# Bank tables for every TensorE step and newly found engine orders in a fused Mamba and local-attention kernel

## What is computed

```python
# Mamba: 256 inner channels, 16 states
u = silu(causal_conv4(x @ in_w + in_b))
delta = softplus((u @ dt1_w + dt1_b) @ dt2_w + dt2_b)
h[t] = exp(delta * A) * h[t-1] + ((exp(delta * A) - 1) / A) * B * u     # for 16 states
y = (sum_n C_n h_n + D * u) * silu(x @ gate_w + gate_b)
x = layernorm(x + y @ out_w + out_b)
# twice (layers l = 0, 1), 8 heads of 64, windows of 64 that see themselves and the one before
q, k, v = split(shift(x) @ wqkv)
q, k = rotary(l2norm(q) * qs, l2norm(k) * ks)
x = x + softmax(mask(q @ k.T)) @ v @ wo
h = layernorm(shift(x)) @ w1 + b1
x = x + (a(h) * gelu(g(h))) @ w2 + b2
x = layernorm(x_in + x)
```

## Time and profile before

| what | value |
|---|---|
| runs, us | 1066.7, 1067.91, 1068.65 |
| median | 1067.91 us |
| span of the profiled execution | 1068.3 us |
| PE busy | 929.2 us, 87% |
| DVE busy | 872.8 us, 82% |
| ACT busy | 786.6 us, 74% |
| POOL busy | 695.8 us, 65% |
| mean granted PE clock | 0.954 |

### The profile page before, as it was taken

The page is one execution under the profiler, slowest core; times in us unless marked ns, Lnnn a source line. Parts: engine busy times, 40 slices in busy tenths (PEclk is TensorE's granted clock), DMA queues, the critical chain, the costliest instruction groups (busy, mean ns, idle before and its releaser), DMA issues. The chain is left out here.

```text
span 1068.3 us, 25986 instructions
## 1 busy us (share of the span) xinstructions
PE 929.2 (87%) x10152; PEld 560.7 (52%) x10152; DVE 872.8 (82%) x1244; ACT 786.6 (74%) x1897; POOL 695.8 (65%) x386
## 2 busy tenths in 40 slices
...
DMA packets 22618, 25.63 MB, mean 24 GB/s; under 512 B 2869, under 2 KB 14815, under 8 KB 22495
## 3 DMA queue, kind: packets, MB, share of 16 engines
...
## 5 line engine op out<-in xcount | busy, mean ns | idle before, releaser
L1062 DVE TENSOR_TENSOR_SCAN scan<-du,decay 128x1028 f32<-128x1028 f32 (+1 forms) x160 | 306.3, 1952 | 10.9 <-PE YY L1252 7.3
L768 POOL TENSOR_TENSOR rn<-ssc,expo 128x16 f32<-128x16 f32 x64 | 214.0, 3344 | 5.3
L764 POOL TENSOR_SCALAR ssc<-ss 128x16 f32<-128x16 f32 x64 | 62.4, 975 | 213.4 <-DVE ss L1119 212.8
L914 ACT ACTIVATE prob<-BB,nmax 128x128 f32<-128x128 f32 x472 | 165.7, 380 | 39.4 <-DVE nmax L1157 28.0
L859 ACT ACTIVATE decay<-delta,negA 128x1024 f32<-128x1024 f32 (+1 forms) x160 | 154.2, 986 | 18.4 <-DVE scan L1062 16.5
L773 POOL TENSOR_TENSOR qkc<-qkc,qks 128x1024 f32<-128x1024 f32 x64 | 159.6, 2493 | 2.8 <-DVE qks L1137 2.7
L1252 PE MATMUL YY<-scan,diag 64*64 64x512 f32 (+1 forms) x1280 | 143.1, 538 | 10.9 <-DVE scan L1062 10.9
L777 POOL TENSOR_TENSOR qkc<-qkc,rn 128x1024 f32<-128x1024 f32 x64 | 133.2, 2082 | 5.0
L1252 PE MATMUL AA<-wqkv,hT 128*128 128x512 f32 x256 | 128.8, 627 | 6.0 <-DVE qks L1137 3.1
L914 ACT ACTIVATION_READ_ACCUMULATOR prob<-BB,nmax 128x1 f32 x472 | 104.2, 221 | 0.0
L1119 DVE TENSOR_REDUCE ss<-sq 128x16 f32<-128x1024 f32 x64 | 77.1, 1205 | 29.6 <-ACT sq L877 29.6
...
## 6 DMA issues: line engine op xcount, KB each, us to landing
...
```

The lines of the kernel that those rows point to most:

```text
L768: pool.tensor_tensor(rn[:, q % 2, :], ssc[:, :], expo[:, 0:2 * HEADS], ALU.pow).then_inc(rn_sb, 1)
L914: ins = act.activation(prob[:, h, :], bank_of(q, a)[:, c * P:(c + 1) * P], ACT.Exp, bias=nmax[:, q % 2, h:h + 1], accum_out=den[:, q % 2, ...
L1062: dve.tensor_tensor_scan(state, step, a, 0.0, ALU.add, ALU.mult).then_inc(scan_sb, 1)
```

## The change

Three things are edited.

**Tables of banks.** HOLDS and LATE go. Each PE step of a kind that needs a pair or a single bank is given its own by a letter in a table: A, B or Y for a pair, C or M for a single bank. Y may be taken once the Mamba part is over. All readers (ACT and DVE) address the bank by the same table. Instructions, their sizes and their number stay as they were.

```diff
+PAIR_TABLES = {
+    "qk_in": "ABBAABBBBBBBBBABBABBABBBAAAAAAAABBBBBBBBAAAAAABAAAABBBYAYYYYAABA",
+    "qk_T": "AAAAABBABABABABBBABAABABBBBBBAAAAABBAABBBBAAAABBAABAYBBBABYYBBAB",
...
+BANK_TABLES = {
+    "layer_T": "CMMMCMMCCCMMMMMCCMMM",
...
-LATE = [q for q in range(TILE.index((0, GROUPS - 1, 0)), len(TILE)) if q % 2]
...
-HOLDS = {"qk_in": "A", "qk_T": "B", "scores": "B", "probs_T": "B", "v_in": "C", "weighted": "C", "out_T": "C",
-         "attn_out": "M", "shift": "M", "norm_T": "M", "layer_T": "M", "up_gate": "AM", "up_a": "M", "down": "M"}
-OWN = {"scores": "qk_T", "probs_T": "scores", "out_T": "weighted"}
+SINGLES = {"layer_T": lambda l, g: QUAD.index((l, g)), "up_a": lambda f, c: NCH * f + c}
+PAIR_STEPS = {name: table.split() for name, table in PAIR_TABLES.items()}
+BANK_STEPS = {name: table.split() for name, table in BANK_TABLES.items()}
...
 def banks_of(step, args):
-    banks = HOLDS.get(step, "")
-    return "Y" if banks == "B" and args[0] in LATE else banks
+
+    pairs, banks = PAIR_STEPS.get(step), BANK_STEPS.get(step)
+    n = nth(step, args)
+    return (pairs[0][n] if pairs else "") + (banks[0][n] if banks else "")
+
+
+OWN = {"scores": lambda q: [("qk_T", (q,))], "probs_T": lambda q: [("scores", (q,))], "out_T": lambda q: [("weighted", (q,))],
+       "shift": lambda f: [("attn_out", (f,))], "norm_T": lambda f: [("shift", (f,))],
+       "down": lambda f: [("up_a", (f, c)) for c in range(NCH)]}
...
-    held, last = {}, {}
+    held, last = {}, {"Y": ("mamba_sum", (GROUPS - 1,))}
...
-            def free(step, *args):
-
-                for last, (f, *rest) in HELD[step, args]:
-                    if last == "attn_out":
-                        pe.wait_ge(x2_sb, f + 1)
...
+            def free(step, *args):
+
+                for last, of in HELD[step, args]:
+                    pe.wait_ge(*release(last, *of))
...
             def qk_T(q):
-                if q == LATE[0]:
-                    pe.wait_ge(m_sum, GROUPS)
```

**Orders.** All five order strings are replaced. The steps are the same ones (848 on PE, 654 on ACT, 710 on DVE, 197 on POOL, 89 on SP); where they stand differs. The planner that wrote the new strings took a DVE scan and a POOL tensor operation to exclude each other in time; nothing in the kernel enforces that. The first steps on DVE:

```diff
 DVE_ORDER = """
-differences 0, step_size 0, scan 0 0, scan 0 1, scan 0 2, scan 0 3, scan 0 4, scan 0 5, scan 0 6, scan 0 7,
...
+differences 0, masks 0, step_size 0, tables 0, scan 0 0, scan 0 1, scan 0 2, scan 0 3, scan 0 4, scan 0 5, scan 0 6,
```

More of the change, by code:

```diff
@@ L94 @@
[L94 to L103, removed]
@@ new lines @@
+1, state_y 2 8, weighted 2, attn_out 0, state_y 2 9, state_y 2 10, scores 3, state_y 2 11, shift 0, state_y 2 12,
+state_y 2 13, probs_T 3, state_y 2 14, state_y 2 15, norm_T 0, out_T 2, up_gate 0, up_a 0 0, mamba_out 2, weighted
+3, u_in 3, out_T 3, up_a 0 1, gate_in 3, up_a 0 2, layer_T 0 2, qk_in 4, v_in 4, rank 3, qk_in 5, step_in 3, down 0,
+v_in 5, attn_out 1, qk_T 4, layer_T 1 0, qk_in 6, scores 4, shift 1, v_in 6, skip 3, state_y 3 0, v_in 7, qk_T 5,
+probs_T 4, state_y 3 1, qk_in 7, scores 5, state_y 3 2, state_y 3 3, weighted 4, norm_T 1, qk_T 6, out_T 4, up_gate
@@ new lines @@
+17, down 3, attn_out 4, out_T 12, state_y 4 6, weighted 13, shift 4, probs_T 14, state_y 4 7, scores 15, state_y 4
+8, out_T 13, qk_T 16, state_y 4 9, weighted 14, qk_in 18, norm_T 4, out_T 14, probs_T 15, v_in 17, state_y 4 10,
+v_in 18, scores 16, weighted 15, state_y 4 11, up_gate 4, up_a 4 0, up_a 4 1, state_y 4 12, out_T 15, up_a 4 2,
+probs_T 16, state_y 4 13, down 4, weighted 16, qk_T 17, qk_in 19, state_y 4 14, scores 17, state_y 4 15, attn_out 5,
+mamba_out 4, qk_T 18, shift 5, out_T 16, u_in 5, probs_T 17, scores 18, v_in 19, weighted 17, layer_T 0 4, gate_in
@@ new lines @@
+probs_T 22, out_T 21, state_y 5 7, qk_T 23, qk_in 25, weighted 22, scores 23, down 6, state_y 5 8, state_y 5 9, v_in
+24, out_T 22, probs_T 23, v_in 25, qk_T 24, weighted 23, state_y 5 10, qk_in 26, state_y 5 11, scores 24, out_T 23,
+state_y 5 12, v_in 26, attn_out 7, probs_T 24, state_y 5 13, qk_T 25, qk_in 27, scores 25, state_y 5 14, state_y 5
+15, weighted 24, shift 7, mamba_out 5, probs_T 25, out_T 24, qk_T 26, u_in 6, scores 26, norm_T 7, v_in 27, gate_in
+6, weighted 25, up_gate 7, up_a 7 0, probs_T 26, layer_T 0 5, qk_T 27, out_T 25, qk_in 28, scores 27, v_in 28,
@@ new lines @@
+8, state_y 6 9, v_in 34, state_y 6 10, down 8, out_T 30, probs_T 31, qk_T 32, qk_in 34, state_y 6 11, scores 32,
+weighted 31, state_y 6 12, state_y 6 13, out_T 31, probs_T 32, attn_out 9, state_y 6 14, state_y 6 15, qk_T 33,
+shift 9, qk_in 35, weighted 32, scores 33, mamba_out 6, out_T 32, v_in 35, norm_T 9, qk_T 34, u_in 7, probs_T 33,
+up_gate 9, gate_in 7, weighted 33, scores 34, layer_T 0 6, out_T 33, qk_T 35, up_a 9 0, v_in 36, qk_in 36, rank 7,
+up_a 9 1, up_a 9 2, probs_T 34, step_in 7, down 9, scores 35, qk_in 37, weighted 34, v_in 37, skip 7, probs_T 35,
```

605 lines of the change are left out of this document (299 added, 306 removed).

## The result

| | before | after |
|---|---|---|
| median, us (range) | 1067.7 (1066.7 to 1068.65) | 1025.4 (1022.72 to 1030.71) |
| ratio, 95% interval | | 0.9619 (0.9588 to 0.9651) |
| span of the profiled execution, us | 1068.3 | 1023.9 |
| its mean granted clock | 0.954 | 0.979 |

The kernel became 42 us faster. The forecast was 1033 us, the range 1006 to 1062. The total came out within 8 us, in part by luck: the waits that the sum was made of gave 21 us and not 35, one term had the wrong sign, and the clock, for which the sum had no term, gave about 18 us.

What follows compares the result with a forecast made beforehand. PE was taken as nearest to the bound, nearly co-bound with DVE in the middle, with 41.6 us of bank waits. Terms -25 - 4 - 3 - 0.9 - 2.4 = -35 took 1068.3 to 1033 us, range 1006 to 1062.

Steps and rivals of the forecast that it cites:

- Bank waits: PE steps held by an unreleased pair or bank: 60% of 41.6 us goes, -25 us, between -8 and -42.
- rival A: Freed PE steps only wait for their data instead: bank term -8 instead of -25, 1050 us; chance 0.17.
- qk_T to scores: `scores` waited 5.4 us for its own `qk_T` copy and now stands further behind: -4 us, between 0 and -5.4.
- Scans against POOL: DVE scans and POOL operations exclude each other; an order keeping them apart saves -3 us, between -13 and +5.
- The opening: Table multiplies and casts before the first scan, `qk_in` 0 ahead of group 1's state steps: -0.9 us, between -8 and +7.
- The end: Last GELU to `down`: with C and M in turn, 5.5 us becomes about 3.1: -2.4, between -1 and -3.5.
- the clock: PE matmuls at the upper clock instead of the lower: little to win in the middle (granted 0.99); no term in the sum.
- B: The release compounds: attention fills the opening (-8) and all bank waits go (-42), 1009 us; chance 0.08.
- C: Pairs with scores stay held until their exponentials are done, stopping PE: slower, 1079 us; chance 0.09.
- D: DVE and ACT alone limit the order, bank waits are only where slack shows: time stays at 1068; chance 0.04.
- DVE must do 639 us in 693, 92%: Check on the middle: DVE's load if 20 of the 35 us gained fall there, which it nearly reached before.
- PE's idle time near 105: Sign that the forecast is right: PE's idle time falls to near 105 us, from 139.

Runs made afterwards that it cites:

- tables_only: Kernel before with its old orders, each step given the pair or bank that comes free first (333 of 648 entries differ): 1042.98 us, ratio 0.9775.
- order_only: New orders of after with the old fixed banks wherever these orders can run with them (66 entries still differ): 1089.39 us, ratio 1.0215.
- new_pairs: Kernel after with its table of pairs kept, but single banks C and M fixed by kind as before (29 entries deviate): 1065.98 us, ratio 0.9981.
- new_singles: Kernel after with its table of single banks kept, but pairs A and B fixed by kind as before (37 entries deviate): 1059.21 us, ratio 0.9912.
- tables_tail: Kernel before with its old orders, banks chosen freely only after the last `mamba_out` (87 entries): 1053.57 us, ratio 0.9867.
- tables_mid: Kernel before with its old orders, banks chosen freely only up to the last `mamba_out` (240 entries): 1068.3 us, ratio 1.0009.
- after_short_rotate: Kernel after with POOL's addition and multiply of `rotate` done on only 128 of 1024 columns: 1017.3 us, ratio 0.953.
- after_half_sums: Kernel after with DVE's sums of squares taken over 32 of each head's 64 values: 1031.45 us, ratio 0.9668.

## Why the prediction was right, and where it wasn't

**Bank waits, -25: the right mechanism, its size in part by luck.** tables_only, the nearest to this term by itself, measured -24.7. But the term was counted in PE's idle time, and of that only 14.6 us went there: 20 us of bank waits (46.0 to 25.6), while the rest grew by 6.5, as rival A says in small. The other 10 us are matmuls at the upper clock. In after, the idle time of the eight kinds fell by 18.6 where 25 was forecast. No run shows why it is less. Rival A in full (waits change their name, -8) falls: `probs_T` waits 6.8 us for exponentials, not more than 9.4. The table of runs says the same: with the new orders, bank waits of 70, 52, 48 and 27 us go with 1089, 1066, 1059 and 1025.

**qk_T to scores, -4: right**, 5.4 to 0.7 us.

**Scans against POOL, -3: wrong in sign.** The step that failed is "an order that keeps them apart can save a part of 13 us". The order doesn't keep them apart: 13 us of stretching became 22. It is the order that does it: the scans sum to 315 to 321 us in after, order_only, new_pairs and new_singles, and to 299 to 306 in before, tables_only, tables_tail and tables_mid. With the norms' multiplies and the casts DVE has some 17 us more to do. What that costs in time is bounded by after_short_rotate, about 8 for all 36 us of stretching; an estimate in proportion, 17 / 36 x 8, gives +4, at the upper end of my range (-13 to +5). Besides, PE now waits 21 us more for scans, which no term had; order_only has 20 of them. What the orders gain lies elsewhere, in the rest of PE's idle time, 82.2 us before and 59.1 after, where no term of mine stood. The largest part of that is `norm_T` behind `ffn_norm`, 11.4 to 2.7 us, and order_only has the 2.7 too.

**The opening, -0.9: inside its range (-5 measured, range -8 to +7), by luck.** "The casts fit in DVE's wait for the softplus" is false: they took 2.03 + 0.96 us instead of 0.22 + 0.42, as POOL's multiply ran beside them, and the first scan starts 3.7 us later, not 1.0. I had costed them by the row of a stretch in which POOL was idle, in the very kernel whose prediction dwells on exclusion. Group 1's `mamba_out` is 9.5 us late (84.2 for 74.7), and group 2's nevertheless 4.8 early (154.9 for 159.7), which fits "not new work, 0 net": what pushed group 1 back was missing ahead of group 2. No run tested that.
The Trainium skill (SBUF — State Buffer, Who interferes with whom) says that casts, too, can run in a mode which takes the port pair that DVE shares with GpSimd, and that whoever issues first keeps it for its whole instruction. The trace agrees for the cast, 2.03 us where 0.22 is its time alone; for the power of the earlier trace rows it doesn't.

**The end, -2.4: right in mechanism, a little small.** From the last GELU to `down` it takes 2.2 us for 3.1 forecast, so -3.3. Another -1.3 is `down` at the upper clock.

**What the sum counted as nothing: the clock.** The prediction named it as one of two ways to win time, and then gave it no term. It was worth about 18 us of PE's busy time. "There is little to win from it in the middle" was right, at most 7.5 us. What failed is the silence on the opening (0.85) and the tail (0.91), where the other 11 lie. How much of that would have been won back by other waits, no run says. Comparing tables_only with after shows it again: 1043.8 - 1023.9 = 20 us of span, of which busy time 919.3 - 906.2 = 13 and idle time 7, at nearly the same bank waits (25.6 and 26.9).

**The sum.** It was 35 against 42 measured, and 44 between the spans. Nearly all of its terms are waits of PE, and PE's idle time fell by 21 and not by 35; PE's busy time fell by 23 where the sum had 0. The mechanism that carried it, freed banks, is the one that the runs show, but that the total came within 8 us is in part two errors that cancel.

**The rivals.** B (1009) asked for a filled opening and no bank waits: the opening gave 5, and 27 us of bank waits are left. C (1079, held by exponentials) fell in after, where `qk_T` never waits for them and `qk_in` about 1 us. Nor is it what makes order_only slow: `qk_T` is held 6.1 us by exponentials there, 6.6 before. D (the tables do nothing) fell with tables_only. "DVE must do 639 us in 693, 92%": it did 650 in 695, and after_half_sums shows that this share alone wasn't the bound.
The check "PE's idle time near 105" gave 118, and "scans over 3 us become few" gave 13 of them where there were 9. Looked at alone, the time would have hidden both.
